# Counting drawn keys with running totals on VectorE in place of one TensorE matmul per key

## What is computed

```
c_sel = c_kv[jnp.arange(b)[:, None, None], indices]      # indices: (8, 256, 64)
kv = (c_sel @ W_kv_up.T).reshape(b, nq, K, 2, H, HD)
scores = jnp.einsum('bqhd,bqkhd->bqkh', q, k) * SCALE
attn = jax.nn.softmax(scores, axis=2)
out = jnp.einsum('bqkh,bqkhd->bqhd', attn, v).reshape(b, nq, d)
```

## Time and profile before

| | |
|---|---|
| median of 3 timed executions | 2637.9 us (2636.37 to 2648.38) |
| profiled execution, its own time | 2646.27 us |
| its span | 2644.5 us |
| mean granted TensorE clock | 0.876 |
| busy over the span | PE 85%, DVE 51%, ACT 38%, POOL 14% |

### The profile page before, as it was taken

How to read it: one execution, slowest core, us unless ns; L and a number is a source line. 1 busy time by engine, 2 the same in 40 slices (tenths; PEclk the granted TensorE clock), 3 DMA queues, 4 the chain that set the end, 5 groups by cost and what they waited for, 6 DMA issues and landing times. The chain is left out here.

```text
span 2644.5 us, 38948 instructions
## 1 busy us (share of the span) xinstructions
PE 2243.5 (85%) x13569; PEld 1574.3 (60%) x13637; DVE 1341.9 (51%) x3927; ACT 998.1 (38%) x3145; POOL 363.0 (14%) x639
## 2 busy tenths in 40 slices
PE   8688898898889988896818588899999999999887
PEld 4356566666677755575704355566666666666655
DVE  7245455564645454322129466665656656566331
ACT  3133535343545443352202135453444444444220
POOL 2044141423232324001000000000000000000000
PEclk9768868877899998897958699998999999999888
DMA  8000000000232210344651000000000000000000
GB/s 296 9 4 1 5 5 9 9 5 9 94 104 83 80 31 29 114 162 172 231 135 48 14 10 1 10 5 5 10 5 10 5 10 5 6 5 5 5 1 9
DMA packets 50763, 116.27 MB, mean 44 GB/s; under 512 B 8192, under 2 KB 30464, under 8 KB 46976
## 3 DMA queue, kind: packets, MB, share of 16 engines
q1 hardware_dynamic: 49024, 109.49, 12.3%
q0 software_dynamic: 1536, 4.20, 0.5%
HBM read 90.20 MB, written 23.46 MB: 43 GB/s over the span
## 5 line engine op out<-in xcount | busy, mean ns | idle before, releaser
L690 ACT ACTIVATE PRS<-PT 128x384 f32<-128x384 f32 (+1 forms) x512 | 265.6, 519 | 847.0 <-PE PT L621 846.4
L753 DVE TENSOR_REDUCE negmax<-SM 128x2 f32<-128x512 f32 x432 | 283.9, 687 | 229.1 <-PE SM L584 121.8
L621 PE MATMUL PT<-const_sb,PRS 128*128 128x128 f32 x1664 | 314.2, 307 | 40.0 <-ACT PRS L690 33.9
L705 ACT ACTIVATE PRS<-SM,negmax 128x128 f32<-128x128 f32 x608 | 248.3, 423 | 142.6 <-DVE negmax L753 142.6
L621 PEld LDWEIGHTS PT<-const_sb,PRS 128*128 128x128 f32 x1664 | 210.1, 155 | 134.9 <-issue 101.4
L2756 DVE TENSOR_SCALAR arena<-arena 128x256 bf16<-128x256 bf16 x1024 | 210.5, 281 | 9.2 <-PE SC L2774 8.2
L574 PE MATMUL SM<-haloU,QM 32*128 32x128 f32 (+1 forms) x1056 | 182.2, 388 | 12.0 <-ACT PRS L705 9.5
L574 PEld LDWEIGHTS SM<-haloU,QM 32*128 32x128 f32 x1056 | 136.5, 223 | 27.3 <-ACT PRS L705 13.0
L574 PE MATMUL SC<-haloU,QM 32*128 32x128 f32 (+1 forms) x480 | 120.0, 408 | 34.6 <-ACT PRS L705 34.6
L2774 PE MATMUL SC<-arena,identb 128*128 128x256 bf16 x1024 | 139.1, 279 | 2.7 <-DVE arena L2756 2.7
L636 PE MATMUL OA<-PRS,big 128*32 128x256 f32 (+1 forms) x1024 | 136.5, 393 | 3.0 <-ACT PRS L690 3.0
(11 more groups left out here) (565 smaller groups left out, 4109.9 us busy)
## 6 DMA issues: line engine op xcount, KB each, us to landing
arena<-lay SPq DMA_DIRECT2D x50, 1024.0 KB, 4.9
arena<-lay SPq DMA_DIRECT2D x1, 7700.5 KB, 21.2
rows<-OT SPq DMA_DIRECT2D x2, 3456.0 KB, 31.9
arena<-lay SPq DMA_DIRECT2D x1, 3862.0 KB, 19.9
arena<-rows SPq DMA_DIRECT2D x25, 128.0 KB, 2.8
arena<-lay SPq DMA_DIRECT2D x25, 128.0 KB, 5.3
rows<-arena SPq DMA_DIRECT2D x25, 128.0 KB, 4.6
rows<-OT SPq DMA_DIRECT2D x1, 2432.0 KB, 21.3
```

What stands on the lines that cost most here:

```text
L621: ins = pe.transpose(bank[:, o:o + P], PR[n % 4][:, t, k * P:(k + 1) * P], ident)
L690: act.activation(dst, src, ACT.Copy).then_inc(S("probs_moved"), 1)
L705: ins = act.activation(dst, src, ACT.Exp, bias=negmax[:, h, r:r + 1], accum_out=rsum[:, t, h:h + 1])
L753: st.post(dve.tensor_reduce(negmax[:, ORDER[s], :], two(banks[s % NB]), AX.X, ALU.max, negate=True), S("max_ready"))
```

## The change

DVE makes two running totals per group in place of 8 separate rows. The first two drawn keys of a group are written as one-hot rows as before. Each of the other six is one `scalar_tensor_tensor`: compare the ramp with the key's index, add the total, write the total. Even keys go to total 0, odd keys to total 1. A new semaphore `hot_step` makes each of the six wait for the instruction two before it. PE sums the two totals of a group: 2 matmuls per group, 32 per batch, where there were 8 and 128. Totals are small whole numbers, exact in bf16. `hot_ready` now counts two per group.

```diff
                 t, j0 = g // 8, g % 8 * 8
+                drawn = [0, 0]
                 for j in range(8):
-                    ins = dve.tensor_scalar(oneh[g % 2][:, j, :], iotab, idx[:, t, j0 + j:j0 + j + 1], None, ALU.is_equal)
-                    st.post(ins, S("hot_ready") if j == 7 else None)
+                    total, index = oneh[g % 2][:, j % 2, :], idx[:, t, j0 + j:j0 + j + 1]
+                    if j < 2:
+                        st.post(dve.tensor_scalar(total, iotab, index, None, ALU.is_equal), S("hot_step"))
+                    else:
+                        dve.wait_ge(S("hot_step"), drawn[j % 2])
+                        st.post(dve.scalar_tensor_tensor(total, iotab, index, total, ALU.is_equal, ALU.add),
+                                S("hot_step") if j < 6 else S("hot_ready"))
+                    drawn[j % 2] = st.count["hot_step"]
                 yield
...
-                pe.wait_ge(S("hot_ready"), GROUPS_HOT * i + g + 1)
-                for j in range(8):
+                pe.wait_ge(S("hot_ready"), 2 * (GROUPS_HOT * i + g + 1))
+                for j in range(2):
                     ins = pe.matmul(SC[:, t * T:(t + 1) * T], identb[:], oneh[g % 2][:, j, :],
-                                    start=j0 + j == 0, stop=j0 + j == NI - 1)
+                                    start=j0 + j == 0, stop=g % 8 == 7 and j == 1)
```

## The result

The changed kernel takes 2711.7 us (median of 4 runs, 2708.7 to 2719.0), the kernel before 2637.1 in the same session: ratio 1.028, 95% interval 1.024 to 1.031. It is slower by 74.6 us and outside the range that was given. The profiled execution of the kernel after spans 2710.7 us, against 2644.5 before.

A forecast was written before the change was run, and what follows sets the result against it. Slots were taken as set by PE, ACT or DVE in turn; 12.5 - 1.9 - 3.6 - 4 x 0.9 - 0.3 = +3 us, 2641 us on the median of 2637.9, range 2618 to 2668.

The forecast's parts named there:

- The new form at a pace of 0.40 us, 1.22 us a group: On DVE, each new instruction was put at 0.40 us for 0.196, adding 1.22 us a group, 157 us in all.
- Six hidden waits cost nothing: On DVE, the six new waits on `hot_step` in each group were costed at nothing.
- DVE sets the slots of batch 0, 6.8 us for 5.08: In batch 0, DVE was to set each two-group slot, 6.8 us for 5.08, +12.5 us for the batch.
- A steady batch, -0.9 us: For each of four steady batches, delays on DVE and savings on PE were to leave -0.9 us at the next tally.
- Batches 1 and 2, -1.9 and -3.6: Batch 1 was to gain 1.9 us, and batch 2, with less side work on DVE, 3.6 us.
- The entry of the count, +1.5 on `hot_ready`: Entering a steady batch's count attention, PE's scores were to wait on `hot_ready`, +1.5 us, behind three nearly back-to-back DVE groups.
- Four late groups a batch count in full, 4 x 0.67 = 2.7 us: Late in a steady batch's count, PE sets the pace and four groups were to save 0.67 us each, 2.7 us.
- 85 us from PE and 157 on DVE cancel: Over the whole kernel, 85 us taken from PE and 157 us put on DVE were to cancel, about +3 us.
- The first: Rival: new form dearer, DVE pace above about 0.44 us, or low clock granted more often; slower, 2671 us at 0.50; chance 0.27.
- The second: Rival: on DVE, bf16 runs two elements a cycle, pace 0.27 us, -32 us, 2606 us; chance 0.10.
- third: Rival: DVE's delay is hidden better and PE's -0.67 us counts in more of the 128 groups, 2624 us; chance 0.13.
- The signs of being wrong: The forecast would fail if the new form's pace is not 0.40, or PE takes low clock through whole tally attentions.

The follow-up runs named there:

- e4: Changed kernel with batch 0 put back to eight rows and eight matmuls, totals only in batches 1 to 7; 2702.4 us, ratio 1.0205 to the kernel before.
- e1: Changed kernel with PE's matmuls put back to eight a group, six of them on rows of zeros; 2710.9 us, ratio 1.027 to the kernel before.
- e9: Kernel before with DVE drawing six of each group's eight rows twice, old instructions, all matmuls kept; 2718.2 us, ratio 1.028.
- e3: Changed kernel with totals and two matmuls only in the last four groups of batches 1 to 7; 2626.2 us, ratio 0.9935 to the kernel before.
- e8: Kernel before with two matmuls for eight in the last four groups of batches 1 to 7, DVE's eight rows kept; 2620.7 us, ratio 0.996.
- e2: Kernel before with two matmuls for eight in every group, DVE's eight rows kept; 2643.9 us, ratio 0.9998.
- e10: Kernel before with two matmuls for eight in batch 0 alone, DVE's rows kept; 2646.6 us, ratio 1.001.

## Why the prediction was wrong, point by point

- **The new form at a pace of 0.40 us, 1.22 us a group.** Right: 0.397, and the group takes 2.85 us for the 2.9 forecast. The choice of the f32 rows of the same shape and scalar was the right one. The rule of the Trainium skill ("Vector Engine (DVE) Microarchitecture Reference", "5.1 Performance modes") agrees; its section 7's reading, by which bf16 would go at 0.27, is not borne out.
- **Six hidden waits cost nothing.** Right: no idle time before the 768.
- **DVE sets the slots of batch 0, 6.8 us for 5.08.** Right by the row: the maxima of the kernel after start at 1537.10 and again at 1543.83, 6.7 us later.

```profile
1537.10 1.28 DVE L753 TENSOR_REDUCE negmax<-SM 128x2 f32<-128x512 f32 x2
...
1538.69 2.46 DVE L2762 SCALAR_TENSOR_TENSOR arena<-arena 128x256 bf16<-128x256 bf16 x6
...
1543.83 1.28 DVE L753 TENSOR_REDUCE negmax<-SM 128x2 f32<-128x512 f32 x2
```

  The stretch from batch 0's scores to batch 1's (1502.9 to 1583.4) is 80.5 us, for 65.0 before (1507.3 to 1572.3): +15.5 where 12.5 was the term, and 9 to 19 by e4, in which batch 0 is undone. The right size.
- **A steady batch, -0.9 us.** This is the step that failed: +10.3. The delay at 2101.34 of 1.22 us came as put where PE has all its matmuls (e1 and e9: +1.2). What I wrote behind it, "PE has 10 us of its own work behind, and the two groups there take off 0.67 each (more where the clock is low): about 0 at 2122", left that work at the clock of the kernel before. It runs at the low clock, from the longer wait on, for two slots: +5.8 us in e9. In the kernel after the delay at that place is +2.8: the scores that I had 0.67 earlier (2094.78) came 0.96 later, since a wait of 1.43 us for ACT ahead of the slot before was followed by low clock from 2128 to 2131, and the two waits below are longer still. At the place of 2101.34:

```profile
2139.70 0.39 PE L2781 MATMUL SC<-arena,identb 128*128 128x256 bf16 x2 [1.33 <-DVE arena L2762]
...
2142.05 1.65 PE L574 MATMUL SM<-KF,QM 32*128 32x128 f32 x8 [1.96 <-ACT PRS L705]
...
2144.80 1.50 PE L636 MATMUL OA<-PRS,VS 128*32 128x256 f32 x8
...
2156.34 1.91 PE L2680 MATMUL PJ<-arena 128*128 128x256 f32 x4
```

  1.33 and 1.96 us of waiting in a row: e1, with all eight matmuls, has 0.67 and 1.29 here. The six matmuls less have made each wait 0.67 longer and bought nothing, since its end is DVE's. Then 1.65, 1.50 and 1.91 us for what takes 0.93, 0.84 and 1.03 at full clock.
- **Batches 1 and 2, -1.9 and -3.6.** Wrong in the same way: +10.5 and +2.7. The count stretch at 1619.3 us takes 62.0 us at a granted clock of 0.86, for 56.6 at 1.00.
- **The entry of the count, +1.5 on `hot_ready`.** The wait was 3.31 us in the kernel after (below, the row at 2177.34) and 1.92 in e9; I had moved only the last of the three groups that stand nearly back to back.

```profile
2177.34 0.39 PE L2781 MATMUL SC<-arena,identb 128*128 128x256 bf16 x2 [3.31 <-DVE arena L2762]
```

- **Four late groups a batch count in full, 4 x 0.67 = 2.7 us.** Nearly right where they are alone: e3 and e8 gain about 16 us of the 19 that seven batches make, 2.0 of 2.7 in a count stretch. In the changed kernel it is drowned: the count is longer, not shorter, its first slots being late and its clock 0.93.
- **85 us from PE and 157 on DVE cancel.** They don't: PE's half is worth 0 in all (e2: 0.9998), and DVE's 157 us of work cost 70. The sum did count PE's half in some slots only; what it lacked was a loss to set against it, since matmuls taken away elsewhere lengthened waits and came with low clock.
- **The rivals.** The first had the sign and, in its last sentences, the cause ("if PE ... is granted the low clock more often"). It had the wrong trigger and no size of its own: the low clock came with waits for DVE, with all of PE's work in place too (e1, e9). The form was not dearer. The second and third fell.
- **The signs of being wrong** named the low clock "through whole tally attentions". It came in parts of them, and that was enough: 0.82 to 0.88 in the steady tallies, where "not much under 0.95" was to show it right.

Open in part: e2 as a whole is at 0.9998 when its late groups alone (e8) gain 0.4%, and its batch 0 (e10) changes nothing that can be told; the remaining groups would have to lose some 10 us, and no kernel had those alone. Their trace shows where it goes. The tallies of batches 0 and 1 take 123.7 us in e2 for 112.1 in the kernel before (117.8 in e10), and the count behind them 64.6 us at a granted clock of 0.82 for 56.6 at 1.00, with 43 matmul records fewer; from there on e2 is 6 us faster. First e2, then the kernel before:

```profile
1627.60:1692.23 64.63, 57.12 (x290) 33.93 (x289) 38.95 (x154) 25.81 (x59) 0.69 (x1) 0.82 0.02 5
1619.34:1675.89 56.55, 50.95 (x333) 33.03 (x336) 38.64 (x152) 25.37 (x58) 0.69 (x1) 1.00 0.02 6
```

The waiting and the low clock were separated by rows and stretches of profiled executions, not by an experiment that keeps the clock up, and what decides how long the clock stays low is open.

## What to carry to other kernels

Work moved from the busiest engine to a half-idle one has to be priced slot by slot: here it paid in the four groups of a batch where the second engine waits for the first, 16 us in all, and lost some 80 us in the others. A wait that grows on TensorE should be priced with work behind it at the low clock too, not with its own length alone: 3 us of waiting went with 3 to 9 us of delay in e9, 7 in the mean. To test such a change, do each half alone; adding only the time to the second engine, with old instructions, gave the whole result.

## What the runs showed of the hardware

- The granted clock fell at 2148 us in e9 right after PE's waits of 0.64 and 1.28 us. In the kernel before it held through the 0.82 us at the same place, fell 5 us later behind one more wait of 0.88, and was back 3.1 us after that. In e9 it came back some 17 us later, 9 us into a run of matmuls without a wait; the 7 us without one from 2148.28 on had not brought it back. Work of PE, matmuls as before, went from 0.93 to 1.59, 0.84 to 1.50 and 1.03 to 1.85 us.
- The kernel before has the same work in each of its steady tallies, and they take 63.7 us at a granted clock of 0.97, 65.3 at 0.95 and 68.5 at 0.90.
- 768 matmuls of 256 columns, 85 us of work at full clock, added to the changed kernel cost nothing that can be told (e1: 2710.9 against 2711.7, some 20 us either way), and the mean granted clock is up from 0.840 to 0.848 in four executions to 0.857 to 0.871 in four.
- A `scalar_tensor_tensor` on 128x256 in bf16 with an index per partition goes at 0.397 us each, the same as f32 (0.40), while `tensor_scalar` in bf16 goes at 0.196.
